# Eight unread products on zeros in the set-up block of a twelve-layer decoder kernel

## The reference

```python
x = _layernorm(x + _L0_attn_ref(x, ...), axis=-1)      # part 0: attention with a line-geometry memory
x = _layernorm(x + _L0_xattn_ref(ctx_1024, x, ...), axis=-1)
x = _layernorm(x + _L0_ffn_ref(x, ...), axis=-1)
...
x = _layernorm(x + _L3_ffn_ref(x, L3_ffn_gate_w, L3_ffn_w1, L3_ffn_w2), axis=-1)
return x
```

## Time and profile before

| | us |
|---|---|
| median of 3 runs | 2971.06 |
| lowest and highest | 2970.99, 2971.61 |
| the profiled execution's own time | 2988.71 |
| span of its trace, first to last instruction | 2987.0 |
| mean granted TensorE clock, as a share of full speed | 0.981 |

### The profile page before, as it was taken

One profiled execution on the slowest core, in us unless ns is written; L12 is line 12 of the kernel. 1 busy time (PEld: TensorE's weight loads), 2 busy tenths in 40 slices (PEclk: granted clock), 3 DMA queues, 4 the chain that ended last, 5 costly groups with the idle time before them and its releaser, 6 DMA issues. The chain is left out here.

```text
span 2987.0 us, 51420 instructions
## 1 busy us (share of the span) xinstructions
PE 2788.8 (93%) x20370; PEld 1797.7 (60%) x20370; DVE 1913.3 (64%) x3469; ACT 1221.3 (41%) x2596; POOL 361.9 (12%) x483
## 2 busy tenths in 40 slices
PE   7999899999998889899999999999898999989898
PEld 4566466666666768566666667766565333346576
DVE  4766377777764247577777753357567999966532
ACT  1333354445532235445554432134242866633211
POOL 1111000000003610000000000122212000001232
PEclk9999999999999989999999999999999999999999
DMA  3001100000012231100000000000000000000241
GB/s 127 17 17 70 44 5 5 5 5 5 13 60 84 81 132 40 44 5 5 5 9 5 37 18 1 28 24 21 19 22 33 18 1 1 1 18 19 105 168 67
DMA packets 43804, 103.54 MB, mean 35 GB/s; under 512 B 4977, under 2 KB 32735, under 8 KB 40241
## 3 DMA queue, kind: packets, MB, share of 16 engines
q1 hardware_dynamic: 37777, 86.66, 8.3%
q0 software_dynamic: 5792, 13.59, 1.5%
HBM read 66.74 MB, written 19.07 MB: 29 GB/s over the span
## 5 line engine op out<-in xcount | busy, mean ns | idle before, releaser
L2732 ACT ACTIVATE prob<-R,neg_max 128x333 f32<-128x333 f32 x512 | 268.4, 537 | 184.3 <-DVE neg_max L2801 184.0
L4239 DVE TENSOR_TENSOR_SCAN arena<-arena,u 128x512 f32<-128x512 f32 x256 | 289.6, 1203 | 0.1
L2620 PEld LDWEIGHTS T<-const,prob 128*128 128x128 f32 (+1 forms) x1536 | 183.8, 143 | 81.8 <-DVE prob L2814 36.4
L2814 DVE TENSOR_TENSOR prob<-prob,rec 128x666 f32<-128x666 f32 x256 | 218.5, 853 | 19.2
L2801 DVE TENSOR_REDUCE neg_max<-R 128x2 f32<-128x666 f32 x256 | 205.9, 846 | 35.2 <-PE R L2609 35.2
L2620 PE MATMUL T<-const,prob 128*128 128x128 f32 (+1 forms) x1536 | 210.9, 274 | 13.1 <-DVE prob L2814 10.8
L2739 ACT ACTIVATE prob_t<-T 128x384 f32<-128x384 f32 x256 | 125.5, 490 | 228.2 <-PE T L2620 222.0
L4170 ACT ACTIVATE arena<-delta,neg_a 128x510 f32<-128x510 f32 x256 | 175.1, 713 | 41.9 <-DVE arena L4239 41.0
L2807 DVE COPY prob_t<-T 128x384 f32<-128x384 f32 x256 | 142.3, 556 | 39.7 <-PE T L2620 13.3
L2539 PE MATMUL O<-keys_in,arena 128*128 128x333 f32 x512 | 164.8, 444 | 0.0
L4073 PE MATMUL R<-arena,diag 64*64 64x512 f32 x1024 | 136.6, 624 | 24.6 <-DVE arena L4239 24.5
(11 more groups left out here) (611 smaller groups left out, 5400.8 us busy)
## 6 DMA issues: line engine op xcount, KB each, us to landing
w<-w_dram SPq DMA_DIRECT2D x16, 1024.0 KB
arena<-pack_dram SPq DMA_DIRECT2D x2, 4100.0 KB, 14.9
q_pad<-q_pad SPq DMA_DIRECT2D x24, 224.0 KB, 2.7
arena<-pack_dram SPq DMA_DIRECT2D x4, 1284.0 KB, 6.7
arena<-pack_dram SPq DMA_DIRECT2D x1, 4896.0 KB, 14.6
slots_in<-x_nat SPq DMA_DIRECT2D x2, 2048.0 KB, 9.7
arena<-planes SPq DMA_DIRECT2D x8, 512.0 KB, 9.6
arena<-k_nat SPq DMA_DIRECT2D x16, 224.0 KB, 2.7
```

What stands on the lines that cost most here:

```text
L2620: last = nc.tensor.transpose(S.T[0:n, i, kc * P:(kc + 1) * P], prob[:, g % 2, i, first:first + n], S.ident)
L2732: last = nc.scalar.activation(prob[:, g % 2, i, :], S.R[:, g % 2, i * BANK:i * BANK + XK], ACT.Exp, bias=neg_max[:, g % 2, i:i + 1], accum ...
L2814: nc.vector.tensor_tensor(prob[:, g % 2, :, :], prob[:, g % 2, :, :], rec[:, g % 2, :].unsqueeze(2).to_broadcast([P, 2, XK]), ALU.mult)\
L4239: nc.vector.tensor_tensor_scan(state[:, q % HELD, :], decay[:, q % DEEP, :], u[:, i % 2, :], 0.0, ALU.mult, ALU.add)\
```

## The change

DVE first sets 512 columns of `ctx_t` to zero and raises a new semaphore. PE, which had no list in the set-up block, gets one: it waits for that semaphore and makes eight products of these zeros with themselves into a bank of `R` that nobody reads. `ctx_t` is loaded only later, by the last transfer of part 0's start.

```diff
 FIRST_BATCHES = 2
+FIRST_PRODUCTS = 8
...
         S.const_in = sem("const_in")
+        zeros_ready = sem("zeros_ready")
...
             @block.vector
             def _(dve):
+                if layers[0] == 0:
+                    nc.vector.memset(S.ctx_t[:, 0, 0:BANK], 0.0).then_inc(zeros_ready, 1)
                 nc.vector.memset(S.x_pad[:, :, N:N + 1], 0.0)
                 if layers[0] != 0:
                     dve.wait_ge(loaded, 32)
                     masks_cast(nc, S)
                 dve.drain().then_inc(set_up, 1)
+
+            @block.tensor
+            def _(pe):
+                if layers[0] == 0:
+                    pe.wait_ge(zeros_ready, 1)
+                    for _ in range(FIRST_PRODUCTS):
+                        nc.tensor.matmul(S.R[:, 0, 0:BANK], S.ctx_t[:, 0, 0:P], S.ctx_t[:, 0, 0:BANK], start=True, stop=True)
```

## The result

| | before | after |
|---|---|---|
| median of 8 runs each, us | 2970.97 | 2976.01 |
| lowest and highest | 2965.67, 2974.53 | 2970.69, 2983.84 |
| profiled execution's span | 2987.0 | 2978.8 |

The changed kernel is slower: ratio 1.0028, 95% interval 1.0019 to 1.0037. The medians are 5.0 us apart; the ratio stands for about 8 us. The forecast was 2974.5 us.

The account below looks back on a forecast made before the run. Part 0's first 30 us were taken as bound by loading that begins when the set-up block ends. Sum: 0 (MEMSET) + 3.4 (release) + 0 (clock in part 0) = +3.4 us on 2971.06, giving 2974.5 us; range 2970.9 to 2979.3.

Parts of the forecast that it names:

- DVE's MEMSET: Set-up block: zeroing 512 columns takes 0.49 us, zeros there at 1.35 us; no cost by itself, 0 in the sum.
- Clock: Set-up block: PE starts at 1.40 us, its clock rises at 6.0 us, and the products on zeros end at 10.7 us.
- The release term: End of the set-up block: first part-0 product moves from 7.63 to 11.0 us, a delay of 3.4 us.
- The release waits for unread products: End of the set-up block: all engines are held until PE's last product, read or not; release 0.3 us later.
- The rival in which it doesn't wait: End of the set-up block: SP starts at 7.6 us as before, delay 0, 2971.1 us; chance 0.07.
- the two on when the clock rises: Zeros' products: no rise in time, 2979.1 us, chance 0.12; or high level from the first product, 2970.5 us, chance 0.07.
- The loads carry it: Part 0's start: SP's transfers stand behind the release, DMA has no slack, so L1851 moves from 36.34 to 39.7 us.
- Gain of the high clock in part 0's start: 0: Part 0's start: faster products gain 0 on the path, because POOL waits for none of them longer than for ctx_t.
- the place that the prediction cites: Part 0: PE idle for 3.78 us before 36.34, then clock down to 0.69, cited as agreeing in kind with the skill.
- Later low stretches: Part 0, low stretch from 37.7 to 41.1 us: up to 1.7 us won or 0.7 us lost; taken as 0.

Follow-up runs that it names:

- twelve products: The changed kernel with 12 products on zeros instead of 8; ratio 1.0052 [1.0037, 1.0067] to the kernel before.
- all loads early: The changed kernel with eight products, SP issuing all of part 0's first transfers in the set-up block, zeros in ctx_hat; 2977.94 us, ratio 1.0036 to before.
- a hold by DVE: The kernel before, no products, with DVE zeroing unused columns in the set-up block so that it ends late; ratio 1.0027 [1.0015, 1.0039].
- three products: The changed kernel with 3 products on zeros instead of 8; 2969.17 us, ratio 1.0007 [0.9995, 1.0019] to the kernel before.
- twin: The kernel before, unaltered under another name; 2969.88 against 2967.66 us, ratio 1.0006 [0.9997, 1.0015].
- both repeated sets: The changed kernel run unaltered a second and a third time against the kernel before; ratios 1.0024 and 1.0030.
- sixteen: The changed kernel with 16 products on zeros instead of 8; 2975.95 us, ratio 1.0027 [1.0014, 1.0039] to the kernel before.
- most loads early: Part 0's first transfers except x_nat and ctx_t issued in the set-up block; ratio to before 0.999 without products, 1.0008 with eight, 0.9997 with three.

## Why the prediction was right and where it was wrong

The sign, the mechanism of the start and the range held (2970.9 to 2979.3 us). The size did not quite: 3.4 us forecast, 5.0 by the medians, and the ratio's middle, 0.28%, is slower by over 0.2%, to which I gave only 0.13. That the median fell so near to the forecast is in part luck: the time held a cost behind part 0 that the sum didn't have. Step by step:

- *DVE's MEMSET*, 0.49 us estimated between two rows: 0.48 measured. PE began at 1.51, not 1.40.
- *Clock.* Rise forecast at 6.0 us. The step from 5.94 to 6.70 is 0.76 us, between 0.86 and 0.43: 0.66 us at the low spacing and the rest at the high one, so it rose at 6.6. Half of the later start and half of the later rise are 0.36 of the 0.45 us by which the end came later, 11.15 instead of 10.7 us. The release term, 3.4 us, became 3.82 by it. That the rise would come 4.6 us after the start of the work was too sharp: from the same start at 1.51 us it came between 4.8 us (twelve products) and 7.0 us (all loads early) by the spacings.
- *The release waits for unread products.* Right: 0.30 us behind PE's last record in every kernel whose products ended last. The rival in which it doesn't wait is gone, and so are the two on when the clock rises, since it rose neither at once nor too late.
- *The loads carry it.* Right: 3.84 us at POOL's wait for `ctx_t`. Taking most of the transfers out from behind the release took the cost away at L1851, and a hold by DVE cost 6.1 us there for 5.8 us of hold, which shows it from both sides. In the time of the whole only the second of the two shows.
- *Gain of the high clock in part 0's start: 0.* Right for the start. PE stood idle for 4.43 us and the clock was low again soon after 20 us. Here the rule of the Trainium skill (TensorE: Matmul & The Clock Gate, "HAM oscillation — how this bites in real kernels"), that the next burst after a wait for DMA starts cold, agrees with the trace in kind only. The wait was for ACT's copy, which itself stood behind the landing of the weights, and the burst did not start cold: L1790 took 1.02 us at 19.56, nearer to the 0.89 of the high level than to the 1.62 of the low one, and the clock fell within it or just behind. The same holds for the place that the prediction cites, where PE started at 36.34 us and the clock fell in 37.5 to 38. The advice of the Trainium skill's same page (table "Why this matters for your kernels") to keep TensorE busy gave nothing in the time here: three products held the high level into part 0 and the time was 1.6 us longer by the medians, within the twin's own difference. What I did not see is that the products would save a low stretch of 3.4 us later in part 0, 1.7 us of time.
- *Later low stretches: "I take 0 and keep both for the range", 1.7 us either way.* **This is the term that was mis-sized.** I had priced one stretch, at 37.7 us. There are some 113 us at the low level in the profiled execution of before (0.019 x 2 x 2987), nearly all of it behind part 0, and any of it can come, go or lengthen. In part 0 one went away, the one at 58 to 61.6 us: 344.2 instead of 346.0 us. The shift of the start isn't its cause, since it is missing with three products too, where nothing is shifted. In parts 1 to 11 it went the other way in two of three traces of eight products, with 117 and 112 us at the low level and 95 in the third, against 91 in the twin; but three products have 111.

How much of the excess over the hold that explains can be worked out roughly. Eight products' mean clock is 0.9802 over both repeated sets against 0.9823. Of this, 0.0017 is the stretch of some 10 us at 20 to 30 us, off the path; before was at the low level too there, but the clock column has no record of it. That leaves 0.0004, some 2.4 us of low level, or 1 us of time. The excess over the hold is 1.2, 3.8 and 5.2 us by the medians of the three sets. So the low stretches account for the spread between executions and for the disorder between eight, twelve and sixteen in direction, but for eight products a part of about 2 us, the size of the twin's own difference, stays open. With most loads early, where eight products cost nothing in part 0, a fourth set leaned the same way, by 4.7 us. Whether eight products meet a worse pattern regularly, or four sets of 7 to 12 executions leaned the same way, wasn't settled. So the cause of the first 3.8 us is shown, up to the features; the cause of what the whole lost beyond it is open.

## What to carry to other kernels

Work that nobody reads is free only where nobody waits for its engine. Look for the next point at which all engines meet, and ask what stands behind it: here it was SP's transfers, and 3.5 us of products past the first loads became 3.8 us of late loads. If a filler is wanted ahead of such a point, size it so that it ends with the wait it fills (three products here), and price it against what is bound there: with the DMA engines busy to 0.98 a faster TensorE had nothing to win in those 20 us. When a program spends about a hundred microseconds at the low clock, in stretches between waits, its later time moves by several microseconds from one execution to the next, so a change of 0.1% at the start is read from the same instruction in both traces, not from the total.

## What the runs showed of the hardware that I had not expected

- SP is held by its own issuing of a transfer. With part 0's eleven first transfers and the two before them issued in a row, the issue of the last lasted 9.70 us, as it had in before (9.88 us) where it cost nothing. SP then came late to the block's end, and all engines with it, at 20.6 us. Holding back the last two brought the block's end back to 8.1 us.
- The column of the granted clock shows nothing of the low level at the program's start: it prints 1.00 for the first 10 us of after, through a spacing of 0.86 us that is the low level's.
- The kernel before takes 2967.6 us on one chip and 2988.84 on another (medians of 35 executions each), with almost the same mean clock, 0.982 and 0.981. In the traces some 19 us of it lie in part 2, 190 to 192 against 169 to 171 us. Why wasn't looked into.
- The same products from the same start don't warm TensorE at the same time: the spacing of the weight loads puts the rise anywhere between 4.8 and 7.0 us in the eight traces with eight or more products, which all start at 1.51 us.
